# Two LoRA layers on one core: A's transposes ahead of the product G, block 0's base product in two halves, and bias and ids by broadcast loads

## What is computed

```python
# layer 0: per batch b, with adapter n0 = itok_B_6_15[b], rank 16
x1 = x + (x @ base_weight.T + base_bias) + (x @ lora_A_w[n0].T) @ lora_B_w[n0].T
# layer 1: per batch b, with adapter n1 = itok_B_3_7[b], rank 16
out = x1 + (x1 @ B[n1].T) @ A[n1].T        # SCALING is 1
```

## Time and profile before

| | before |
|---|---|
| median of 3 runs | 100.53 us (100.04 to 100.63) |
| profiled execution | 100.39 us, of which the span 98.3 us |
| TensorE matmuls busy | 92.7 us (94%) |
| VectorE / ScalarE / GpSimd busy | 64.5 / 57.6 / 59.4 us |
| DMA | 19.12 MB, mean 195 GB/s |
| chain that ended last | TensorE 81%, DMA 6%, VectorE 4%, ScalarE 2% |

### The profile page before, as it was taken

The page is one execution under the profiler, slowest core; times in us unless marked ns, Lnnn a source line. Parts: engine busy times, 40 slices in busy tenths (PEclk is TensorE's granted clock), DMA queues, the critical chain, the costliest instruction groups (busy, mean ns, idle before and its releaser), DMA issues.

```text
span 98.3 us, 2329 instructions
## 1 busy us (share of the span) xinstructions
PE 92.7 (94%) x672; PEld 90.9 (92%) x672; DVE 64.5 (66%) x124; ACT 57.6 (59%) x191; POOL 59.4 (60%) x125
## 2 busy tenths in 40 slices
PE   5997999999699999999999999999999999999980
PEld 5986989999599999999999999999999999999970
DVE  3397992249127758687776958687775958686360
ACT  2263636196676669394856749494765749490210
POOL 6504899000575999988595957658595957708500
PEclk9999999999999999999999999999999999999998
DMA  1999999927796089959997389995537274520205
GB/s 57 373 335 324 273 386 301 248 58 201 222 210 237 5 259 225 285 184 259 219 282 210 75 221 253 226 243 205 117 127 196 63 225 47 202 107 0 107 0 213
DMA packets 15873, 19.12 MB, mean 195 GB/s; under 512 B 1109, under 2 KB 11221, under 8 KB 15702
## 3 DMA queue, kind: packets, MB, share of 16 engines
q1 hardware_dynamic: 14576, 13.71, 47.5%
q0 software_dynamic: 1280, 5.28, 21.8%
q10 hardware_dynamic: 6, 0.00, 0.0%
HBM read 13.14 MB, written 5.84 MB: 193 GB/s over the span
## 4 chain that ended last, share of the span: by engine, by line
PE 81%; DMA 6%; DVE 4%; ACT 2%; issue 1%; SPq 1%; DVEq 0%; ACTq 0%
PE psum L409 53%; PE psum L446 11%; DMA b_rows<-in_L_cond_B 6%; PE psum L377 4%; PE psum L438 4%; PE psum L455 4%; DVE table_rounded L630 3%; PE psum L392 2%; PE psum L478 2%; ACT wd L541 1%; PE psum L420 1%; SPq L201 1%; PE psum L397 1%; DVE b_cols L694 1%; DVE y L669 1%
## 5 line engine op out<-in xcount | busy, mean ns | idle before, releaser
L409 PE MATMUL psum<-wd,xt 128*128 128x256 f32 (+1 forms) x384 | 61.4, 309 | 0.0
L409 PEld LDWEIGHTS psum<-wd,xt 128*128 128x128 f32 x384 | 55.6, 188 | 0.1
L541 ACT ACTIVATE wd<-table_rounded 128x128 fp32r x128 | 28.0, 300 | 16.7 <-PE psum L409 14.0
L330 POOL TENSOR_TENSOR up_rows<-gathered_rows,up_rows 128x512 fp32r<-128x512 f32 x16 | 20.6, 1290 | 14.8 <-ACT up_rows L541 14.8
L313 POOL DMA_INDIRECT gathered_rows<-by_rank,rows x16 | 15.9, 996 | 10.8 <-DMA by_rank<-row_ends 8.2
L630 DVE TENSOR_TENSOR xt<-psum,xt 128x512 fp32r<-128x512 f32 x16 | 11.1, 691 | 9.4 <-ACT xt L541 7.7
L637 DVE STREAM_TRANSPOSE psum<-x_squares 128x512 f32<-128x512 f32 x13 | 14.4, 1110 | 0.0
L446 PE MATMUL psum<-up_rows,u_sel 128*128 128x256 f32 x96 | 14.2, 284 | 0.0
L323 POOL TENSOR_TENSOR g_sel<-gathered_rows,batch_mask 128x16 f32<-128x16 f32 x64 | 12.2, 227 | 1.6 <-DMA gathered_rows<-by_rank,rows 1.4
L446 PEld LDWEIGHTS psum<-up_rows,u_sel 128*128 128x128 f32 x96 | 12.8, 190 | 0.3
L649 DVE STREAM_TRANSPOSE psum<-psum 128x128 f32<-128x128 f32 x16 | 5.3, 331 | 11.4 <-PE psum L409 8.7
(11 more groups left out here) (66 smaller groups left out, 71.3 us busy)
## 6 DMA issues: line engine op xcount, KB each, us to landing
out<-y SPq DMA_DIRECT2D x15, 256.0 KB
x_squares<-in_x SPq DMA_DIRECT2D x8, 256.0 KB
w_rows<-in_L_cond_base_weight SPq DMA_DIRECT2D x2, 512.0 KB, 3.7
bw_rows<-in_L_cond_lora_B_w SPq DMA_DIRECT2D x1, 1024.0 KB, 8.4
a_rows<-in_L_cond_lora_A_w SPq DMA_DIRECT2D x1, 1024.0 KB, 11.3
by_rank<-bw_by_rank SPq DMA_DIRECT2D x4, 256.0 KB
x_squares<-in_x SPq DMA_DIRECT2D x8, 128.0 KB
x_rows<-in_x SPq DMA_DIRECT2D x3, 256.0 KB, 10.8
```

The source lines that it names most:

```text
L330: nc.gpsimd.tensor_tensor(out=up_rows[:, k % 2, LO, :], in0=gathered_rows[:, k % GATHERS, 0:D], in1=up_rows[:, k % 2, HI, :], op=ALU.subtr ...
L409: last = nc.tensor.matmul(bank_of(k, half)[:, start:end], xt[:, k % 2, c, x_part, :], wd[:, w_part, c, col:col + end - start], start=(c == ...
L541: return nc.scalar.activation(dst, src, ACT.Copy)
```

## The change

- Loads: x of block 0 moves between the two halves of w, x of block 1 ahead of A. Bias (2 KB to 128 partitions, 256 KB written) and ids (twice 32 KB) are loaded by broadcast from ScalarE's queue after w's high parts; the two matmuls and VectorE's memsets for them are gone.
- `w_chunks`: GpSimd copies chunks 0 to 2, VectorE chunk 3.
- TensorE: `base(0)` is cut by halves. Half 0 comes right after b1's transposes, half 1 now carries D (so `EDGE_U` is gone) and stands behind G. A's transposes stand ahead of G. c1 chunks 2 and 3 stand behind bw.
- ScalarE: G's copy to `row_ends` moves behind A's four copies and the first `select` of layer 0.
- VectorE, GpSimd: the low parts follow; the row numbers come after `a1_by_rank` and the bias product; the register loads of `g_select` stand ahead of its waits.
- Block loop: in block 2 half 0 comes first in one piece, and `up(1)` moves into block 3.

```diff
-            for half in range(2):
+            load_w(0)
+            load_x(0)
+            load_w(1)
...
-            load_x(0)
+            load_x(1)
             sp.dma_start(a_rows[:, :, :], lora_a.rearrange("(g n) r d -> (n r) g d", g=C)).then_inc(a_in, 16)
-            load_x(1)
             load_x(2)
...
+            for oc in range(C - 1):
+                pool.wait_ge(w_plus, oc + 1)
+                nc.gpsimd.tensor_copy(w_chunks[:, oc, :, :],
+                                      w_rows[:, oc, :].rearrange("p (m c) -> p c m", c=C)).then_inc(w_chunked, 1)
...
+                n1 = adapters_of(pool, k, L1)
                 pool.wait_ge(gathered[k % GATHERS], 16 * (k // GATHERS) + 16)
                 if k >= 2:
                     pool.wait_ge(gh_filled, k - 1)
-                n1 = adapters_of(pool, k, L1)
...
+            act.dma_start(bias_all[:, :], bias.rearrange("(a n) -> a n", a=1).to_broadcast([P, D])).then_inc(bias_in, 16)
...
+            wait_x(0)
+            wait_drained(pe, "w1")
+            base(0, range(C), halves=[0])
...
+            wait_drained(pe, "a3")
             wait_d(0)
-            for c in range(C):
-                for n, (x_part, d_part) in enumerate(HALVES):
-                    last = nc.tensor.matmul(EDGE_U, xt[:, 0, c, x_part, :], wd[:, d_part, c, D_AT[0]:D_AT[0] + P],
-                                            start=(c == 0 and n == 0), stop=(c == C - 1 and n == 2))
-            last.then_inc(u_filled, 1)
+            base(0, range(C), halves=[1])
             wait_x(1)
             x_fill(2)
-            wait_drained(pe, "a3")
+            wait_drained(pe, "c1_1")
             wait_d(1)
             base(1, range(C))
 
 
             wait_x(2)
+            base(2, range(C), halves=[0])
+            add_gh(0)
             wait_d(2)
-            pe.wait_ge(u_blocks_ready, 1)
-            base(2, [0])
-            add_gh(0)
-            base(2, [1])
+            base(2, [0, 1], halves=[1])
             up(0)
-            base(2, [2])
+            base(2, [2, 3], halves=[1])
             add_gh(1)
-            base(2, [3])
-            up(1)
...
-            for h in range(2):
+            c1_high(0)
+            xt_high(1)
+            c1_high(1)
...
             select(0, L1, first[0, L1])
-            xt_high(0)
             select(1, L1, first[1, L1])
-            wait_filled(act, "g")
-            copy(row_ends[:, 0:N0 * R // P, 0:P], fill_of("g").rearrange("p (g m) -> p g m", m=P)).then_inc(act_drained, 1)
             for g in range(4):
                 wait_filled(act, f"a{g}")
                 copy(table0_rounded[:, g * 8:g * 8 + 8, HI, :, :], by_adapter(g)).then_inc(act_drained, 1)
-            xt_high(1)
             wait_drained(act, "a3")
             select(0, L0, first[0, L0])
+            wait_filled(act, "g")
+            copy(row_ends[:, 0:N0 * R // P, 0:P], fill_of("g").rearrange("p (g m) -> p g m", m=P)).then_inc(act_drained, 1)
             select(1, L0, first[1, L0])
```

More of the change, by code:

```diff
@@ L360, in w_fill @@
                 last.then_inc(filled, 1)
-            for oc in range(C):
-                w_fill(oc)
-            pe.wait_ge(b1_in, 16)
-            for c in range(C):
-                last = nc.tensor.transpose(fill_of("b1")[:, c * P:(c + 1) * P], b1_rows[:, c * P:(c + 1) * P],
-                                           ident[:, :])
-            last.then_inc(filled, 1)
-            pe.wait_ge(ids_f_ready, 3)
-            nc.tensor.matmul(fill_of("ids")[:, 0:2 * B], ones[:, :], ids_f[:, :, :],
-                             start=True, stop=True).then_inc(filled, 1)
             def c1_chunk(c):
@@ L380, in c1_chunk @@
                     last.then_inc(filled, 1)
-            wait_drained(pe, "b1")
-            pe.wait_ge(w_chunked, C)
-            c1_chunk(0)
-            c1_chunk(1)
-            wait_drained(pe, "ids")
-            c1_chunk(2)
-            pe.wait_ge(bw_in, 16)
-            for q, earlier in enumerate(("b1", "w0", "w1", "w2")):
-                wait_drained(pe, earlier)
-                for r in range(4):
-                    last = nc.tensor.transpose(fill_of(f"bw{q}")[:, r * P:(r + 1) * P], bw_rows[:, :, 4 * q + r],
-                                               ident[:, :])
-                last.then_inc(filled, 1)
-            c1_chunk(3)
-            pe.wait_ge(bias_in, 16)
-            nc.tensor.matmul(fill_of("bias"), ones[:, :], bias_row[:, :], start=True, stop=True).then_inc(filled, 1)
             def base(k, chunks, with_d=True, halves=range(2)):
@@ L450, in up @@
                         last.then_inc(out_filled, 1)
+            for oc in (0, 1):
+                w_fill(oc)
+            x_fill(0)
+            for oc in (2, 3):
+                w_fill(oc)
+            pe.wait_ge(b1_in, 16)
+            for c in range(C):
+                last = nc.tensor.transpose(fill_of("b1")[:, c * P:(c + 1) * P], b1_rows[:, c * P:(c + 1) * P],
+                                           ident[:, :])
+            last.then_inc(filled, 1)
+            wait_x(0)
+            wait_drained(pe, "w1")
+            base(0, range(C), halves=[0])
+            wait_drained(pe, "b1")
+            pe.wait_ge(w_chunked, C)
+            c1_chunk(0)
+            c1_chunk(1)
+            pe.wait_ge(bw_in, 16)
+            for q, earlier in enumerate(("b1", "w0", "w1", "w2")):
+                wait_drained(pe, earlier)
+                for r in range(4):
+                    last = nc.tensor.transpose(fill_of(f"bw{q}")[:, r * P:(r + 1) * P], bw_rows[:, :, 4 * q + r],
+                                               ident[:, :])
+                last.then_inc(filled, 1)
+            x_fill(1)
+            wait_drained(pe, "w3")
+            c1_chunk(2)
+            c1_chunk(3)
+            pe.wait_ge(a_in, 16)
+            for g, earlier in enumerate(("bw1", "bw2", "bw3", "c1_0")):
+                wait_drained(pe, earlier)
+                for c in range(C):
+                    last = nc.tensor.transpose(fill_of(f"a{g}")[:, c * P:(c + 1) * P],
+                                               chunk(a_rows[:, g, :], c), ident[:, :])
+                last.then_inc(filled, 1)
             wait_drained(pe, "bw3")
@@ L503, in _ @@
                 base(k, [0])
+                if k == 3:
+                    up(1)
+                    base(k, [1])
                 add_gh(k - 1)
-                base(k, range(1, C))
+                base(k, range(2 if k == 3 else 1, C))
                 up(k - 1)
@@ L613, in _ @@
             up_high(1)
+            select(3, L1)
             u_high(1)
-            select(3, L1)
             up_high(2)
```

106 lines of the change are left out of this document (45 added, 61 removed).

## The result

The changed kernel takes 102.56 us (median of 4 runs, 101.96 to 102.75) against 100.40 us (100.04 to 100.63) before: ratio 1.0208, 95% interval 1.0152 to 1.0265. It is slower by 2.2 us. A second measurement, beside other kernels on another chip, gave 103.11 against 100.30, ratio 1.0286 (1.0233 to 1.0339). The forecast was 101.2 with the range 99.6 to 102.6. The time lies inside the range by 0.04 us, at its slow end, and the second measurement lies outside it: that the range held is luck as much as judgement.

The account below looks back on a forecast made before the run. TensorE was taken to bound the block loop, so only the end of up(2) counted: 42.3 against 41.55, +0.75 on 100.39, gives 101.1; with 0.14 for the median, 101.2 us was predicted, range 99.6 to 102.6.

Parts of the forecast that it names:

- a table that comes too late: G's copy to row_ends, then store and gather 0, come late, so add_gh(0) can start only at 33.3 us.
- two named places: TensorE waits ahead of base half 1 (1.8 us) and ahead of add_gh(0) (2.1 us).
- the hold of 0.45: At w's diagonal, VectorE's additions wait 0.45 us for GpSimd's second w_chunks copy; bounds 0 and 1.0.
- the load of w's second half: Early loads: x's 256 KB ahead of it cost 0.65 us, so it lands at 6.05 instead of 5.4.
- ScalarE's row of work: ScalarE's order from c1 through layer 1 selects, A's copies and layer 0 selects to G's copy: 16.75 to 23.35 us.
- 2.67 us later: G's copy on ScalarE, now behind four layer 0 selects, starts at 23.35 us where it stood at 20.68.
- The store and the gather: Behind G's copy: store issued 0.68 us after its start, 4.13 more until gather 0 at 28.15; rows land at 32.45.
- Rival B: Table's store lands as quickly as x loads (2.6 us, not 4.13): all behind 1.5 us earlier, 99.7 us; chance 0.17.
- The register load: GpSimd's register load, now ahead of g_select's wait, gives back some 0.65 us before g_select(0).
- Rival C: Loads come later: bw_rows, with 0.15 us to spare, delays TensorE's c1; 1.0 us late gives 102.2; chance 0.16.
- Rival D: TensorE's clock halves after the 2.1 us wait ahead of add_gh(0): end 1.8 us later, 103.0; chance 0.10.
- 0.14 for the median: Addition to the sum: the earlier kernel's median of 100.53 us lay 0.14 above its profiled execution.

Follow-up runs that it names:

- the part alone in the kernel before: Kernel before the change, with only the load of x of block 0 put between w's halves: 102.09 us, ratio 1.0157 to the kernel before.
- the halves together: Changed kernel with x of block 0 loaded behind w's second half again: 102.72 us, ratio 1.0258 to before; later versions keep this load order.
- copies in turn: Kernel with G first, filled wait, w loaded together, GpSimd's w copies after the additions; its a1 copy now also waits for bw_by_rank: 99.62 us, ratio 0.9924.
- G product first: Changed kernel with A's transposes back behind the product G, on TensorE and in ScalarE's drains: 101.96 us, ratio 1.0121 to before.
- G's copy ahead of the selects: Changed kernel with ScalarE copying G to row_ends before the four selects of layer 0: 101.80 us, ratio 1.0149 to before.
- the versions with G first: Changed kernel with G ahead of A again: 101.96 us; with block 1 filling the wait 100.68; with w together and copies after additions too, 99.49.

## Why the prediction was right and where it was wrong

**The structure of the sum was right.** The change was to be slower by a table that comes too late, with TensorE standing still at two named places. Both are in the profile: 1.61 us ahead of base half 1 (forecast 1.8) and 1.77 ahead of `add_gh(0)` (2.1), the latter released by `g_sel`. `up(2)` ended at 43.13, not 42.3, so the working was short by 0.83 us. The change costs time as forecast, but the size was missed: +0.75 us of span forecast, +1.58 measured. Step by step:

| step | forecast | after |
|---|---|---|
| additions to the diagonal begin (6.1 and the hold of 0.45), end | 6.55, 7.05 | 7.26, 7.75 |
| base half 0 | 9.05 | 9.65 |
| c1 through, ScalarE takes it | 16.75 | 17.22 |
| first select of layer 0 | 22.55 | 23.14 |
| base half 1 | 23.7 | 24.30 |
| G's copy | 23.35 | 23.95 |
| gather 0 | 28.15 | 28.48 |
| `g_select(0)` | 32.5 | 33.02 |
| `add_gh(0)` | 33.3 | 33.91 |
| `up(2)` ends | 42.3 | 43.13 |

**The term that was mis-sized is the load of w's second half.** I priced x's 256 KB at half of what 512 KB cost, 0.65 us, so 6.05; it landed at 7.23. Of this error of 1.2 us, 0.49 is a term left out: the issue of x stands ahead in SP's queue, so that the second half is issued at 1.80 and not at 1.3, and each issue is 0.44 to 0.45 us long. The rest is the load, which took 5.4 us from its issue where 4.1 and 0.65 were allowed. The error of 1.2 entered the sum as 0.6 to 0.7, since I had added 0.45 for a hold that did not occur there: the additions came after GpSimd's two copies, not during them. Two wrong terms met, one too small and one in vain. Everything from base half 0 to G's copy is then late by 0.5 to 0.6. With the part alone in the kernel before, the second half landed 2.2 us later. With the halves together it landed 4.1 to 4.3 us after its issue, against 5.4 to 6.4 with x in between (seven traces each). Why the load itself takes at least 1.1 us longer, nearly twice the share of 256 KB, isn't settled by these runs.

**ScalarE's row of work and the position of G's copy** were right to 0.1 us relative to each other: 0.81 from the first select to G's copy (forecast 0.8), 1.16 to TensorE's start (1.17). The move of the copy alone took 1.07 us off the wait. The step "2.67 us later" for G's copy measured 3.27, of which the late w is 0.6.

**Behind G's copy** small errors went both ways. The copy was 0.60 late; the store gave 0.27 back, so that gather 0 was 0.33 late; the gather's landing and the start of `g_select(0)` took 0.19 more, TensorE's start 0.09, and the way to the end of `up(2)` 0.22, since `add_gh(2)`, priced at 0.22, took 0.46 behind a stop of TensorE.

**The store and the gather** were right within 0.3: 3.85 us from the store's issue to the gather (4.13 forecast), 4.1 to 4.3 in the other versions where the table was waited for. **Rival B** falls: the store took 2.98 us to land in the profile after and 3.3 to 3.4 in the others whose chain shows it, never 2.6. B was also priced too high. Each time 0.87 us went by between the store's landing and the gather's start, so the 4.13 was no landing time, and a store that landed in 2.6 would have saved some 0.7 us, not 1.5. The register load was worth 0.57 (forecast 0.65), shown by its being put back.

**The hold between VectorE and GpSimd** is real and stood at the wrong place. In the profile after, it shows where I had not looked, in VectorE's scaling of the ids beside GpSimd's bias product:

```profile
17.98 0.96 DVE L713 TENSOR_SCALAR ids_all_f<-ids_all 128x128 f32<-128x128 int32 x1
```

```profile
17.57 1.29 POOL L279 TENSOR_TENSOR bias_b_terms<-b_rows,bias_all 128x512 f32<-128x512 f32 x1 [0.75 <-DMA bias_all<-in_L_cond_base_bias]
```

0.96 us, ending at 18.94, behind GpSimd's 18.86; the same line took 0.22 in the version with copies in turn, where nothing ran beside it. Here it cost nothing, since A's first low part came at 20.48.

**Rival C** was right in kind and wrong in the load: `bw_rows` was in at 11.2, well before TensorE came to it at 12.95, and the broadcasts delayed nothing that was waited for. It was w that was late. **Rival D** did not happen in the profile after; the wait of 1.77 kept the clock at 1.00. Three of the changed kernel's nine executions, one in the first and two in the second measurement, had a mean clock of 0.983, and the span of G product first grew by 1.1 from 98.8 with that clock. So D belongs to the median, not to the profile, as part of the 0.6 us by which the median exceeds the profiled execution. The rest is not shown: the others at full clock had spans up to 101.0 and no profile, and later loads, as in the profile of G's copy ahead of the selects, would do it. The forecast also carried the spread of the kernel before over: it added 0.14 for the median, where the changed kernel's median lies 0.6 above its profiled execution.

**The range and the chances.** Slower by over 1%, which came true, had a chance of 0.42, against 0.44 for no change. The forecast of 101.2 stood 0.3 us below the limit of 101.5, and the late load, 0.6 in the sum, crossed it by itself. How much higher the chance should have been, one result can't tell.

## What to carry to other kernels

When a product is moved behind other work, follow what hangs on it: the copy that drains it, and here 4 us of store and 4.4 of gather behind the copy. TensorE did G 3.8 us later than before and its copy came 3.3 later. Taking the copy out from behind the selects gave back 1.1 of the wait; the rest went in the versions with G first again. When a load is moved ahead of another, count its issue in the queue as well as its bytes. A saving on the busiest engine arrives only if every load and every side table is as early as before; count the waits that open in place of the work removed. And work that was given to GpSimd to free VectorE cost time here when it ran while VectorE added or copied in SBUF.

## What the runs showed of the hardware that I had not expected

- A load of 256 KB put between two of 512 KB on one queue moved the issue of the second from 1.31 to 1.80 us, and its landing from 4.1 to 4.3 us after the issue to 5.4 to 6.4, an amount that changed from run to run.
- VectorE and GpSimd held each other up for whole instructions, in both directions, where VectorE's inputs lay in SBUF: a GpSimd conversion of sixteen elements took 1.02 us beside a VectorE copy and 0.20 without; a VectorE copy took 4.38 instead of 1.04 beside a GpSimd copy of 3.81; an addition 1.23 instead of 0.28. VectorE's four copies out of PSUM were not held: 2.48 us beside a GpSimd copy of 3.77, 2.47 with none beside them.
- The granted clock fell to 0.50 behind a wait of 3.05 us and to a mean of 0.59 behind one of 2.64; it stayed at 1.00 behind one of 2.57, and at 1.00 from 9 to 12 us behind one of 2.00 (G's copy ahead of the selects). Behind one of 1.90 it fell to 0.50 from 8 to 10 us (x between w's halves in the kernel before). The length of the single wait did not decide it.
